# A decoder layer and a non-local block on one core: row-block turns spread over slots 3 to 5, a row statistics moved to slot 6, and ScalarE's large loads moved behind the last exponential of a slot

## The reference

```python
def attention(q, k, v, mask):                       # 16 heads of 32
    scores = jnp.einsum('bhqd,bhkd->bhqk', q, k) / jnp.sqrt(jnp.float32(HD))
    scores = scores * mask - 10000.0 * (1.0 - mask)
    return jnp.einsum('bhqk,bhkd->bhqd', jax.nn.softmax(scores, axis=-1), v)
...
ln_out = layernorm(hidden_states, ln1_s, ln1_b)
q, k, v = jnp.split(ln_out @ w_qkv + b_qkv, 3, axis=-1)
x = hidden_states + merge_heads(attention(q, k, v, ltor_mask)) @ w_ao + b_ao
q = layernorm(x, ln2_s, ln2_b) @ w_q + b_q
k, v = jnp.split(encoder_states @ w_kv + b_kv, 2, axis=-1)
x = x + merge_heads(attention(q, k, v, cross_mask)) @ w_co + b_co
x = x + gelu(layernorm(x, ln3_s, ln3_b) @ w1 + b1) @ w2 + b2
# then the non-local block, per sequence, with x as (256 channels, 512)
W = theta(x)^T phi(context) / 512
y = w_w @ (W @ g(context)^T)^T ; out = batchnorm(y) + x
```

## Time and profile before

| | |
|---|---|
| median of 3 runs | 2007.74 us (2007.12 to 2007.95) |
| the profiled execution | 2011.13 us, its span 2009.3 us |
| granted TensorE clock, mean | 0.999 of full speed |
| PE busy | 1976.2 us, 98% |
| DVE busy | 1470.8 us, 73% (in the attention part 90% and more) |
| ACT busy | 1162.6 us, 58% |
| DMA | 252.67 MB, 681720 packets, 533312 of them under 512 B |

### The profile page before, as it was taken

How to read it: one execution, slowest core, us unless ns; L and a number is a source line. 1 busy time by engine, 2 the same in 40 slices (tenths; PEclk the granted TensorE clock), 3 DMA queues, 4 the chain that set the end, 5 groups by cost and what they waited for, 6 DMA issues and landing times. The chain is left out here.

```text
span 2009.3 us, 41550 instructions
## 1 busy us (share of the span) xinstructions
PE 1976.2 (98%) x13632; PEld 1570.0 (78%) x13632; DVE 1470.8 (73%) x3868; ACT 1162.6 (58%) x3251; POOL 550.2 (27%) x556
## 2 busy tenths in 40 slices
PE   9999999999999999999999998999999999999998
PEld 8877777777776777777777776888888888888887
DVE  7799999999999999899899888564444343435333
ACT  4388878888888888888888788421111121212111
POOL 1012222222224344323423432053132131313000
PEclk9999999999999999999999999999999999999999
DMA  8546667567668867767767734531212212121201
GB/s 279 168 94 139 146 165 155 128 168 161 135 173 193 195 172 173 168 162 180 176 152 183 170 90 116 171 107 35 79 42 68 68 47 78 47 63 52 61 24 48
DMA packets 681720, 252.67 MB, mean 126 GB/s; under 512 B 533312, under 2 KB 626112, under 8 KB 681536
## 3 DMA queue, kind: packets, MB, share of 16 engines
q1 hardware_dynamic: 535616, 195.84, 38.5%
q10 hardware_dynamic: 145920, 54.55, 11.2%
HBM read 167.41 MB, written 82.84 MB: 125 GB/s over the span
## 5 line engine op out<-in xcount | busy, mean ns | idle before, releaser
L1309 ACT ACTIVATE A_p<-A_p,A_nmax 128x256 f32<-128x256 f32 x1024 | 507.1, 500 | 5.4 <-DVE A_res L1634 1.7
L1666 DVE CUSTOM_DVE_ANT_0 A_p<-A_p,A_ma 128x256 f32<-128x256 f32 x1024 | 376.6, 423 | 4.6
L1656 DVE TENSOR_TENSOR A_p<-A_sc,A_mk 128x1024 f32<-128x1024 f32 x256 | 312.3, 1220 | 48.0 <-PE A_tp L1071 47.4
L820 POOL TENSOR_TENSOR A_ct_l<-A_cx,A_ct_h 128x256 fp32r<-128x256 f32 x122 | 114.3, 937 | 652.3 <-DVE A_nmax L1666 639.1
L1368 ACT ACTIVATE A_pt<-A_tp 128x512 f32<-128x512 f32 x396 | 218.5, 588 | 47.2 <-PE A_tp L1071 45.9
L1071 PEld LDWEIGHTS A_tp<-A_ident,A_p 128*128 128x128 f32 x1584 | 178.8, 141 | 71.2 <-ACT A_p L1309 33.0
L1071 PE MATMUL A_tp<-A_ident,A_p 128*128 128x128 f32 x1584 | 222.5, 277 | 1.5 <-DVE A_xt_l L1617 0.7
L1505 ACT ACTIVATE A_mk<-A_tp,A_cols 128x512 f32<-128x512 f32 x62 | 42.8, 690 | 269.1 <-PE A_tp L68 269.0
L1309 ACT ACTIVATION_READ_ACCUMULATOR A_p<-A_p,A_nmax 128x1 f32 x1024 | 197.2, 193 | 0.0
L1505 ACT ACTIVATE A_ma<-A_tp,A_cols 128x512 f32<-128x512 f32 x62 | 42.8, 690 | 242.5 <-PE A_tp L68 242.5
L66 PE MATMUL A_banks<-A_xt_h,A_w_h 128*128 128x512 f32 x384 | 162.2, 422 | 3.4 <-DVE A_res L1634 2.1
(11 more groups left out here) (248 smaller groups left out, 5001.7 us busy)
## 6 DMA issues: line engine op xcount, KB each, us to landing
exponentials<-A_ln_shift SPq DMA_DIRECT2D x464, 64.0 KB, 2.7
A_pt<-exponentials SPq DMA_DIRECT2D x116, 256.0 KB, 3.1
A_rt<-inverses SPq DMA_DIRECT2D x512, 32.0 KB, 2.4
x<-A_res SPq DMA_DIRECT2D x64, 256.0 KB, 3.6
A_res<-x ACTq DMA_DIRECT2D x58, 256.0 KB, 4.1
turned<-A_x ACTq DMA_DIRECT2D x224, 64.0 KB, 2.8
A_x<-x SPq DMA_DIRECT2D x54, 256.0 KB, 3.7
A_x<-x ACTq DMA_DIRECT2D x42, 256.0 KB, 3.1
```

Source lines behind the costliest of these rows:

```text
L820: pool.tensor_tensor(ct_l[:, f, part], cx[:, :], f32(ct_h[:, f, part]), ALU.subtract).then_inc(c_lo, 1)
L1309: act.activation(p[:, g % 2, j, t, :], p[:, g % 2, j, t, :], ACT.Exp, scale=-1.0, bias=nmax[:, g % 2, j, t:t + 1], accum_out=rsum[:, g % 2 ...
L1656: dve.tensor_tensor(p[:, g % 2, heads, :, :].rearrange("p j t s -> p j (t s)"), sc[:, heads, :], m, ALU.mult)\
L1666: dve.tensor_tensor_reduce(out=a_, in0=a_, in1=ma[:, b, t, :], scale=-1.0, scalar=BIG, op0=ALU.add, op1=ALU.min, accum_out=nmax[:, g % 2, ...
```

## The change

In slot 3 one row-block turn is done instead of two (tile 0), in slot 4 two (tiles 1 and 2), and in slot 5 one (tile 3), this one at the slot's very end, after the output of `b_`. The writes follow: tile 0 with the exponentials 0 to 3 of slot 4, tile 1 with 0 to 3 of slot 5, tile 2 with 4 to 7 of slot 5, tile 3 with 0 to 3 of slot 6. The row statistics of tile 0 moves from slot 0 of the next block into slot 6 (end of the slot), for blocks 2 and up. ScalarE's loads of rows, context, masks and residual rows are issued behind exponential 7 of their slot (or behind exponential 0 of the next), and some of them in another slot: row tiles 1, 2 and 3 in slots 6, 7 and 0 rather than 0, 0 and 1; residual rows 0 and 1 in slots 0 and 3 rather than both in slot 2; 2 and 3 in slot 6 and at the start of slot 7. Block 15 keeps its early residual loads.

```diff
+    EARLY_ADDS = (NU - 1,)
...
-                if by_blocks(k) and h in (4, 5):
-                    write_block(k, r, 2 * h - 8 + n // 4, n % 4)
+                tile = {(4, 0): 0, (5, 0): 1, (5, 1): 2, (6, 0): 3}.get((h, n // 4))
+                if by_blocks(k) and tile is not None:
+                    write_block(k, r, tile, n % 4)
...
-                if by_blocks(k - 1) and (h, n) in ((0, 3), (0, 4), (1, 3)):
-                    load_row(k + 1, r + 1, 2 * h + n - 2)
-                if NB <= k + 1 < NU and n == 4 and h in (1, 2):
+                if by_blocks(k) and (h, n) in ((6, 7), (7, 7)):
+                    load_row(k + 2, r + 2, h - 5)
+                if by_blocks(k - 1) and (h, n) == (0, 7):
+                    load_row(k + 1, r + 1, 3)
+                if NB <= k + 1 < NU and n == 7 and h in (1, 2):
                     load_context(r + 1, h - 1)
-                if NB <= k < NU and (h, n) == (3, 5):
+                if NB <= k < NU and (h, n) == (3, 7):
                     load_mask(r, 1)
-                if NB <= k < NU - 1 and (h, n) == (7, 3):
+                if NB <= k < NU - 1 and (h, n) == (7, 7):
                     load_mask(r + 1, 0)
-                if 1 < k < NU and h == (2 if k < NU - 1 else 0) and n in (5, 6):
-                    load_res(k - 1, r - 1, n - 5)
-                if 0 < k < NU and h == 6 and n in (5, 6):
-                    load_res(k - 1, r - 1, n - 3)
+                if 1 < k < NU and (h, n) in (((0, 7), (3, 7)) if k not in EARLY_ADDS else ((0, 5), (0, 6))):
+                    load_res(k - 1, r - 1, int((h, n) in ((3, 7), (0, 6))))
+                if 0 < k < NU and (h, n) in ((6, 7), (7, 0)):
+                    load_res(k - 1, r - 1, h - 4)
...
-                if k == 2 and (h, n) in ((1, 5), (2, 3), (3, 3), (6, 4)):
-                    load_o_copy(min(h - 1, 3))
+                if k == 2 and (h, n) in ((1, 5), (2, 7), (4, 7), (5, 7)):
+                    load_o_copy({1: 0, 2: 1, 4: 2, 5: 3}[h])
...
+            def row_blocks(r, t):
+                dve.wait_ge(ln_x, (r + 1) * TT + (t + 1))
+                dve.transpose(x[:, t, :], x[:, t, :]).then_inc(a_blk, 1)
...
-                if by_blocks(k) and h in (3, 4) or k == NU - 1 and 3 <= h < 3 + TT:
-                    for t in (2 * h - 6, 2 * h - 5) if by_blocks(k) else (h - 3,):
-                        dve.wait_ge(ln_x, (r + 1) * TT + (t + 1))
-                        dve.transpose(x[:, t, :], x[:, t, :]).then_inc(a_blk, 1)
+                if k == NU - 1 and 3 <= h < 3 + TT:
+                    row_blocks(r, h - 3)
+                if by_blocks(k):
+                    for t in {3: (0,), 4: (1, 2)}.get(h, ()):
+                        row_blocks(r, t)
                 if k < NU and h in ((0, 1) if k else (1, 2)):
-                    row_statistics(r + 1, 0 if h == (0 if k else 1) else 2)
+                    if h != 0 or k < 2:
+                        row_statistics(r + 1, 0 if h == (0 if k else 1) else 2)
                     row_statistics(r + 1, 1 if h == (0 if k else 1) else 3)
...
+                if by_blocks(k) and h == 5:
+                    row_blocks(r, 3)
+                if by_blocks(k) and h == 6:
+                    row_statistics(r + 2, 0)
```

## The result

The change makes the kernel slower: 2021.09 us median (2019.06 to 2022.12, 6 runs) against 2007.85 us (2006.35 to 2009.31, 6 runs), a ratio of 1.0064 (95% interval 1.0051 to 1.0076). The forecast was 2003.0 and its range ended at 2012. The profiled execution took 2021.2 us with a span of 2019.3, against 2011.1 and 2009.3 before, so the traces differ by 10 us and the medians by 13.

The account below looks back on a forecast made before the run. TensorE, busy 98% of the span, was taken to bound the kernel. Gains of 8.1 us (7.1, 0.7, 0.3) less costs of 3.4 (2.1, 1.3) gave 2007.7 - 4.7 = 2003.0 us; eight-in-ten range 1998.5 to 2012.

Parts of the forecast that it names:

- What bounds the kernel: TensorE, busy 98% of the span, sets the time; its waits for `k_l`, 8.5 us at slot 4, can be won.
- one turn less in slot 3: 0.65 us leaves VectorE's list ahead of k3's output, shrinking 13 waits at the start of slot 4: gain 7.1 us.
- The loads that leave slot 2: Two residual loads go to slots 0 and 3, so slot 2's inverses meet less traffic: gain 0.3 us in slot 4.
- Slot 1 of block 8: One tile's statistics leave slot 0 ahead of k0's output, shortening the 1.03 us wait there: gain 0.7 us.
- The turn in slot 5 and the statistics in slot 6: Both fit on VectorE, whose next masks wait over 1 us for TensorE: cost 0.
- The writes that come into slot 6: Tile 3's four writes push the exponentials' load at slot 6's start: cost 0.15 us per block, 2.1 us in all.
- The inverses of slot 6: A later load delays slot 7's scaling, seen as `res` waits at slot 0: cost 1.3 us, bounds -2 and +10.
- The later residual loads give back half a load: In slot 6, residual loads issued later perhaps return half a load of DMA time against the writes; counted within their 2.1 us.
- The second rival: Slot 6 overflows, delaying exponentials and inverses; 14 us lost against 8.1 gained, 2013.6 us; chance 0.19.
- the wait for `res` over 10 us: Sign of the second rival: the weight loads' (PEld's) wait for `res`, 4.4 us before, goes over 10.
- A_pt over 8: Sign of the second rival: PE's wait for A_pt goes over 8 us; the forecast had about 2 growing to 4.

Follow-up runs that it names:

- e10: Kernel before, with only the turn of tile 1 in slot 3 moved behind the low half of k; ratio 0.9978 to the kernel before.
- e1: Changed kernel with turns two and two in slots 3 and 4 and writes in slots 4 and 5 again; ratio 1.0019 to the kernel before.
- e14: Changed kernel with turns two and two, writes in slots 4 and 5, and row tile 1 loaded in slot 0 again; ratio 0.9997 to the kernel before.
- e4: Changed kernel with only the row statistics of tile 0 back in slot 0; ratio 1.0066 to the kernel before.
- e5: Kernel before with only the changed kernel's turns (one, two, one in slots 3 to 5) and late writes; ratio 1.0024 to the kernel before.
- e8: Kernel before with only the writes moved: tiles 1 and 2 in slot 5, tile 3 in slot 6; ratio 1.0047 to the kernel before.
- e12: Kernel before with only row tile 1 loaded behind the last exponential of slot 6 instead of the fourth of slot 0; ratio 1.0038.
- e3: Changed kernel with only residual tiles 2 and 3 loaded behind the sixth and seventh exponential of slot 6 again; ratio 1.0057 to the kernel before.
- e6: Kernel before with only the turns changed, to one in slot 3 and three in slot 4; ratio 1.0059 to the kernel before.
- e15: e10 plus the change's statistics and loads, but row tile 1 in slot 0 and residual tile 3 behind the fifth exponential of slot 7; ratio 1.0054.
- e13: e8 with tile 3's four writes in runs of 512 bytes instead of 128, same bytes, outputs permuted; ratio 1.0017 to the kernel before.

## Why the prediction was wrong

- *What bounds the kernel*, and *one turn less in slot 3*: right. 7.1 us plus 0.3 was foretold, slot 4 gives 8.0 (and 0.6 more in block 1, which the table leaves out), `k_l` falls to 0.4 (foretold below 3), the weighings over slot 4 are 8.9 to 9.0 apart, and e10 has 7.3 of it by the order of two instructions alone.
- *The loads that leave slot 2*, 0.3: right as what is left beside the turn, but the loads are worth far more than the text says: slot 4 loses 5.0 us less with both turns in slot 3 (e1, e14), as it loses 7.3 less by the turn without the loads (e10). Both reach for the same 8 us. That slots 2 and 3 gave 0.8 is not their work: slot 3 loses 0.1 or nothing in every other row, with the loads moved or not.
- *Slot 1 of block 8*, 0.7: slot 1 gave 1.0, but by luck. The text gives it to the statistics that leave slot 0; e4 puts them back, and block 8 still loses nothing there.
- *The turn in slot 5 and the statistics in slot 6*, 0: right for the statistics (e4). The turn makes ScalarE wait 1.77 us at the start of slot 6 in block 5, and 26.6 us in 15 pieces over the kernel where it waited 0.6 before. Slot 6 shows nothing of it (5.1 in e5, 5.8 in e8). Whether the 2.8 us that slot 7 has more in e5 than in e8 are its work was not separated.
- *The writes that come into slot 6*, 2.1: slot 6 lost 3.7 in all. The landing of the exponentials (6.6) and TensorE's wait (4.5) came as written. The size was near, taken for itself.
- *The inverses of slot 6*, 1.3 us with an upper bound of 10: this is the step that failed. Slots 7 and 0 lost 16.3 us. The mechanism was in the text (VectorE has no room in slot 7, the delay shows as `res` at slot 0), and two things in it were wrong. The row load of 256 KB that the change adds behind the last exponential of slot 6 had no term at all; e12 prices it at 7.6 us, by way of the inverses' load back (2.8 us to landing instead of 2.2), where the text looked at their store alone. The writes were costed by the share of the engines that they take, and their effect on a 16 KB store that waits behind them was taken near the lower end because one row had a wait of 0.26, on another transfer; e8 prices them at 9.4, of which slot 6 has 3.2.
- *The later residual loads give back half a load*: e3 shows slot 6 better by 2.3 and slot 7 worse by 4.0. Together they give nothing back.

The second rival holds, by the sign that the text gave for it (the wait for `res` over 10 us: 13.5), while its other sign (A_pt over 8) did not come (4.5): it put 0.7 of 1.0 us per block on the exponentials in slot 6, and most of the overflow leaves the slot by way of the inverses. Its price of 14 us was too low; 20 were lost in slots 6, 7 and 0.

## What to carry to other kernels

When a stretch has its DMA engines full, list every transfer that the change adds to it or moves within it, and follow the small ones that others wait for, there and back: here the store of 16 KB of inverses took 0.9 us longer to land, and a load of 256 KB issued beside their load back held that up by 0.6 us. The 256 KB of the exponentials still just fitted in most blocks (TensorE's wait for them is 4.5 us in 8 pieces). Before a move that needs DMA moved too, look for one that only swaps two instructions on the late engine: that had nearly all of the gain in slot 4 (e10), and the kernel became faster. And when an operation is moved later, look through each engine's list for what waits for it in order (ScalarE's writes in e6, GpSimd's bias in e15).

## What was not expected of the hardware

One load of 256 KB in each of 14 blocks, moved from slot 0 to the end of slot 6, costs 7.6 us (e12). The late writes cost 9.4 us (e8), and 3.4 with the last tile's in runs of 512 instead of 128 bytes, at the same bytes (e13). And a bubble may not be all loss: in e6, where TensorE stands 1.2 us in slot 5 of block 5, slot 0 loses 1.8 us over the blocks instead of 4.7. That the transfers catch up in the bubble would explain it; no run tests that.
